# Keys of the second layer and keys and values of the third made inside feed-forward sections

## The reference, cut to what matters

```
# second layer (weights L1_*): pruned attention, then a ternary feed-forward
kh = heads(ctx @ Wk.T + bk);  vh = heads(ctx @ Wv.T + bv)
p  = softmax(qh kh^T / 4); the 14 keys with the least column sum are dropped
x  = x + concat(p vh) @ Wo.T + bo
x  = x + bitlinear(gelu(bitlinear(layernorm(x), w1, b1)), w2, b2)
# third layer (L2_*): masked attention
K = heads(ctx @ Wk.T + bk);   V = heads(ctx @ Wv.T + bv)
p = softmax(where(mask, Q K^T / 4, -1e9));  x = x + concat(p V) @ Wo.T + bo
```

## Time and profile before

| what | us |
|---|---|
| median of 3 runs (lowest, highest) | 1206.9 (1205.46, 1210.3) |
| the profiled execution's own time | 1207.3 |
| its span | 1205.3 |
| PE busy | 1015.1 (84%) |
| DVE busy | 900.0 (75%) |
| ACT busy | 755.9 (63%) |
| POOL busy | 238.1 (20%) |

### The profile page before, as it was taken

How to read it: one execution, slowest core, us unless ns; L and a number is a source line. 1 busy time by engine, 2 the same in 40 slices (tenths; PEclk the granted TensorE clock), 3 DMA queues, 4 the chain that set the end, 5 groups by cost and what they waited for, 6 DMA issues and landing times. The chain is left out here.

```text
span 1205.3 us, 28063 instructions
## 1 busy us (share of the span) xinstructions
PE 1015.1 (84%) x9190; PEld 824.6 (68%) x9190; DVE 900.0 (75%) x2541; ACT 755.9 (63%) x2804; POOL 238.1 (20%) x426
## 2 busy tenths in 40 slices
PE   3999967578999976667999978999998993888885
PEld 3788855246777753446777758999997982666663
DVE  4789868786888868995777765566556984788884
ACT  2787887577777868885777753112113552688884
POOL 1233310002222212332223210000001111333331
PEclk8899998858999997887999999999998996799998
DMA  7340000000000000004232000000000100000002
GB/s 241 92 143 17 14 1 1 1 9 15 14 13 13 10 2 1 0 0 106 76 87 62 13 2 1 1 0 0 0 1 18 32 23 1 1 2 0 0 1 70
DMA packets 44426, 32.64 MB, mean 27 GB/s; under 512 B 16184, under 2 KB 43456, under 8 KB 44352
## 3 DMA queue, kind: packets, MB, share of 16 engines
q1 hardware_dynamic: 44352, 31.72, 8.8%
HBM read 23.32 MB, written 2.10 MB: 21 GB/s over the span
## 5 line engine op out<-in xcount | busy, mean ns | idle before, releaser
L783 ACT ACTIVATE L1a_pr<-L1a_scores,L1a_nm 128x128 f32<-128x128 f32 x256 | 93.1, 417 | 13.5 <-DVE L1a_nm L857 13.5
L783 ACT ACTIVATE L2a_pr<-L2a_scores,L2a_nm 128x128 f32<-128x128 f32 x256 | 90.9, 392 | 5.8 <-DVE L2a_nm L857 5.8
L783 ACT ACTIVATE L3f_pr<-L3f_scores,L3f_nm 128x128 f32<-128x128 f32 x256 | 90.5, 403 | 3.3 <-DVE L3f_nm L857 3.3
L783 ACT ACTIVATE L0a_pr<-L0a_scores,L0a_nm 128x128 f32<-128x128 f32 x256 | 90.9, 392 | 2.3 <-DVE L0a_nm L857 2.3
L783 ACT ACTIVATION_READ_ACCUMULATOR L1a_pr<-L1a_scores,L1a_nm 128x1 f32 x256 | 65.5, 256 | 0.0
L783 ACT ACTIVATION_READ_ACCUMULATOR L3f_pr<-L3f_scores,L3f_nm 128x1 f32 x256 | 62.4, 244 | 0.0
L2145 POOL TENSOR_TENSOR x_all<-x_all,L3a_xnorm 128x256 f32<-128x256 f32 x16 | 11.9, 743 | 253.6 <-DVE L3a_nm L2164 253.6
L857 DVE TENSOR_REDUCE L2a_nm<-L2a_scores 128x4 f32<-128x512 f32 x64 | 42.2, 682 | 25.2 <-PE L2a_scores L644 25.2
L1789 PE MATMUL L2f_inner<-L2f_taT,L2f_loraBT 128*128 128x128 f32 x512 | 59.7, 275 | 0.9 <-DVE L2f_hs L1941 0.9
L1778 PEld LDWEIGHTS L2f_inner<-L2f_xTb,L2f_wiT 128*128 128x128 f32 x512 | 58.3, 192 | 1.5 <-ACT L2f_loraBT L1745 1.2
L1778 PE MATMUL L2f_inner<-L2f_xTb,L2f_wiT 128*128 128x128 f32 x512 | 58.6, 275 | 0.9 <-ACT L2f_loraBT L1745 0.9
(11 more groups left out here) (550 smaller groups left out, 3050.7 us busy)
## 6 DMA issues: line engine op xcount, KB each, us to landing
setup_ctx_nat<-in_ctx SPq DMA_DIRECT2D x4, 512.0 KB, 5.5
x_all<-in_x SPq DMA_DIRECT2D x1, 2048.0 KB, 12.4
L0a_ctxT<-ctxT_all SPq DMA_DIRECT2D x16, 128.0 KB, 2.0
L_ffn_w_w<-in_L_ffn_w SPq DMA_DIRECT2D x2, 1024.0 KB, 7.0
L1a_ctxT<-ctxT_all SPq DMA_DIRECT2D x16, 128.0 KB, 2.0
L2a_ctxT<-ctxT_all SPq DMA_DIRECT2D x16, 128.0 KB, 2.0
L3a_mem<-in_ctx SPq DMA_DIRECT2D x16, 128.0 KB, 2.0
out<-x_all SPq DMA_DIRECT2D x1, 2048.0 KB, 7.5
```

The costliest lines, as they stand in the source:

```text
L783: ex = act.activation(pr[q.s][:, j, h, :], S[j][:, h * P:h * P + P], ACT.Exp, bias=nm[q.s][:, j, h:h + 1], scale=-1.0, accum_out=ls[q.s][: ...
```

## The change

- L0f: TensorE transposes the second layer's Wk at the section's start, VectorE copies it and splits the bias row bk into three bf16 rows (`BiasRows.vector`, placed ahead of the normalization of x). After slots 5, 8, ..., 20 TensorE makes the keys of two sequences each (`project_keys`: for each sequence four products in f32 and two in bf16 that add the bias), the last four sequences' keys after slot 23; ScalarE copies each pair's keys (128x512) to SBUF. ScalarE's square root for the layer norm goes ahead of its weight scaling.
- L1a: no `project_k`, `add_k` or transposed Wk; `kbd` comes from the stored keys. The rounding of the ternary weights is split: `scale` after `drop_eight`, `clip` where `add_k` was, `round` after `add_q`.
- L1f: Wk and Wv of the third layer are transposed after the ternary weights, the 512-wide bias row is split on VectorE ahead of the first normalization, and in each pair step TensorE makes keys and values of two sequences (`keys_values`) into one bank `KV`, which ScalarE copies (128x512) twice in a step (`take_kv`). That bank comes out of `T2`: three banks A, B, C now hold the transposed h of both streams, and stream 1 waits until ScalarE has taken stream 0's. TensorE's loop is written out.
- L2a: no `project_k`, `project_v`, `add_k`, no context copies; `add_v` is a copy from the stored values; SyncE issues all later loads without waits. Wk and Wv aren't transposed here.
- First-layer weights, the eight-bit weights and, later, the stored keys and values share one SBUF area (`arena`).

```diff
 # L1a, vector
                         piece(prev, drop_eight)
+                        if cur:
+                            beside.scale(dve, cur.b)
                         piece(last, norm_out)
                         piece(prev, drop_rest)
                         piece(nxt, add_k)
+                        if cur:
+                            beside.clip(dve, cur.b)
                         piece(last, add_out)
                         piece(nxt, add_q)
+                        if cur:
+                            beside.round(dve, cur.b)
                         piece(prev, keep_values)
...
-                    if kind == PRUNED and cur:
-                        beside.round(dve, cur.b)
 # the bias, vector
+        dve.memset(self.parts, 0.0).then_inc(self.s, 1)
+        dve.wait_ge(self.s, n)
+        src = self.row
+        for k, at in enumerate((0, 32, 64)):
+            dve.tensor_copy(piece, src).then_inc(self.s, 1)
...
+            dve.tensor_copy(self.parts[at:at + 1, :], piece[at:at + 1, :])
+            ins = dve.tensor_tensor(rest, src, piece, ALU.subtract)
...
 # L0f, tensor
+                def project_keys(m, bank):
...
+                    for s in range(NS):
+                        for j in range(DC):
+                            out = bank[:, s * D + j * P:s * D + j * P + P]
+                            for c in range(DC):
+                                pe.matmul(out, WkT[:, c, j * P:j * P + P], g.ctxT[:, NS * m + s, c, :],
+                                          start=(c == 0), stop=False)
+                            mm = bias.keys(pe, g, out, j * P)
+                    mm.then_inc(s_k_ps, 1)
...
                         mm.then_inc(s_gu_ps, 1)
-                    if i == 0:
-                        pe.wait_ge(s_t_sb, NL + FLAT)
+                        if FC0 * i + f in key_slots:
+                            project_keys(key_slots[FC0 * i + f], banks[6])
+                pe.wait_ge(s_h, FC0 * NG - 2)
+                for n in range(2):
+                    project_keys(6 + n, banks[n])
 # L1f, scalar
                             act.activation(hh[s][:, :], hp[s][:, :], ACT.Gelu).then_inc(s_gelu[s], 1)
+                            if nxt and s == 0:
+                                take_kv(nxt, 0)
+                    if nxt and not cur:
+                        take_kv(nxt, 0)
...
                     if old:
                         turn_back(old, 1, 0).then_inc(s_qT[1][1], 1)
+                    if nxt:
+                        take_kv(nxt, 1)
 # L1f, tensor
+                def keys_values(b):
+                    if b:
+                        pe.wait_ge(s_kv, b)
+                    for j in range(DC):
+                        out = KV[:, j * P:j * P + P]
+                        for c in range(DC):
+                            pe.matmul(out, WkT[:, c, j * P:j * P + P], g.ctxT[:, b, c, :], start=(c == 0), stop=False)
+                        bias.keys(pe, g, out, j * P)
+                    out = KV[:, D:2 * D]
+                    for c in range(DC):
+                        pe.matmul(out, g.ctxT[:, b, c, :], WvT[:, c, :], start=(c == 0), stop=False)
+                    bias.values(pe, g, out, D).then_inc(s_kv_ps, 1)
+
                 def step(old, cur, nxt):
+                    if nxt:
+                        keys_values(nxt.b(0))
                     if old:
                         for s in range(NS):
                             pe.wait_ge(s_scaled[1][s], old.v)
                             pe.wait_ge(s_x[s], old.v)
+                            if s == 1:
+                                pe.wait_ge(s_qT[1][0], old.v)
...
                                 mm = pe.transpose(XT[s][:, c * P:c * P + P], xs[s][:, c * P:c * P + P], g.ident[:, :])
                             mm.then_inc(s_qT_ps[0][s], 1)
+                        keys_values(nxt.b(1))
```

More of the change, by code:

```diff
@@ L443, with attention @@
 COPIES = {PLAIN: "vvav", PRUNED: "aaaa", MASKED: "vvav", MIXED: "vvav"}
-def attention(nc, g, name, kind, w, turned, needs, later=(), beside=None):
+def attention(nc, g, name, kind, w, turned, needs, later=(), beside=None, keys=None, vals=None):
     sec = Section(nc, name)
@@ L601, in project, with bank_free @@
                     return mm
-                def project_k(q, new, prev):
+                def bank_free(q, new, prev):
                     if new:
@@ L743, in fill @@
                 def fill():
[L744 to L748, removed]
+                    for k in ("Wk", "Wv"):
+                        if turned and k in turned:
+                            turn_weight(k)
+                    if not no_k:
+                        w_turned(pe, "Wk")
+                        project(w["Wk"], g.ctxT[:, 0]).then_inc(s_k_ps[0], 1)
                     for s, bank in ((0, T[1]), (1, G)):
@@ L1138, in factors, with scale, clip, round @@
         dve.reciprocal(self.inv, self.mean.unsqueeze(2).to_broadcast([P, 2, NB // 2]))
-    def round(self, dve, k):
+    def scale(self, dve, k):
         row, scale = self.rows[:, k, :], self.inv.rearrange("p w k -> p (w k)")[:, bass.ds(k, 1)]
         dve.tensor_scalar(row, row, scale, MAGIC, ALU.mult, ALU.add).then_inc(self.s_scaled, 1)
+    def clip(self, dve, k):
+        row = self.rows[:, k, :]
         dve.wait_ge(self.s_scaled, k + 1)
         dve.tensor_scalar(row, row, MAGIC + 1.0, MAGIC - 1.0, ALU.min, ALU.max).then_inc(self.s_clipped, 1)
+    def round(self, dve, k):
         dve.wait_ge(self.s_clipped, k + 1)
-        dve.tensor_scalar(self.rounded[:, k, :], row, MAGIC, None, ALU.subtract)
-def fake_quant_ffn(nc, g, w, q8, q3):
+        dve.tensor_scalar(self.rounded[:, k, :], self.rows[:, k, :], MAGIC, None, ALU.subtract)
+class BiasRows:
+    def __init__(self, nc, sb, name, width):
+        self.width = width
+        self.row = sb(f"{name}_row", [P, width])[:, :]
+        self.parts = sb(f"{name}_parts", [P, width], BF16)[:, :]
+        self.s = nc.alloc_semaphore(f"{name}_split")
+    def vector(self, dve, rest, piece):
+        n = 1
+        dve.memset(self.parts, 0.0).then_inc(self.s, 1)
[3 more added lines that the diff above has]
+            dve.tensor_copy(piece, src).then_inc(self.s, 1)
+            n += 1
+            dve.wait_ge(self.s, n)
+            dve.tensor_copy(self.parts[at:at + 1, :], piece[at:at + 1, :])
+            ins = dve.tensor_tensor(rest, src, piece, ALU.subtract)
+            ins.then_inc(self.s, 1)
+            n += 1
+            dve.wait_ge(self.s, n)
+            src = rest
+        self.count = n
+    def keys(self, pe, g, out, lo):
+        return pe.matmul(out, self.parts[0:96, lo:lo + P], g.onesb[0:96, :], start=False, stop=True)
+    def values(self, pe, g, out, lo):
+        return pe.matmul(out, g.onesb[0:96, :], self.parts[0:96, lo:lo + D], start=False, stop=True)
+def fake_quant_ffn(nc, g, w, q8, q3, Wk, bias, keys):
     sec = Section(nc, "L0f")
@@ L1253, in _, with take_keys @@
                 load_table(act, g, ACT.Silu)
+                def take_keys(m, bank):
+                    act.wait_ge(s_k_ps, m + 1)
+                    act.copy(keys[:, NS * m:NS * m + NS, :, :], bank[:, :].rearrange("p (b c t) -> p b c t", b=NS, c=DC)
+                             ).then_inc(s_k, 1)
                 for i in range(NG):
@@ L1386, in _, with bitlinear_ffn @@
                 sweep_pairs(pe, step)
-def bitlinear_ffn(nc, g, w, q3):
+def bitlinear_ffn(nc, g, w, q3, wkv, bias, both):
     sec = Section(nc, "L1f")
@@ L1472, in _, with take_kv @@
                              .rearrange("p (m n) -> p m n", m=4)).then_inc(s_t_sb, 1)
+                for n, (dst, bank) in enumerate(((WkT, A), (WvT, B))):
+                    act.wait_ge(s_kw_ps, n + 1)
+                    act.copy(dst[:, :, :], bank[:, :].rearrange("p (c n) -> p c n", c=DC)).then_inc(s_kw, 1)
+                def take_kv(q, s):
+                    act.wait_ge(s_kv_ps, NS * q.v + s - 1)
+                    act.copy(both[:, q.b(s), :], KV[:, :]).then_inc(s_kv, 1)
                 def turn_back(q, s, m):
```

176 lines of the change are left out of this document (131 added, 45 removed).

## The result

The kernel after takes 1245.3 us (median of 4 runs, 1242.4 to 1248.0), the kernel before 1208.2 beside it (4 runs): ratio 1.031, 95% interval 1.0275 to 1.0341. It is slower, as forecast, but by 37 and not by 22, and 5 above the end of the range. The profiled execution has a span of 1243.1, 37.8 more than before.

The account below looks back on a forecast made before the run. The prediction took the chain of engines setting each section's pace as the bound, reading one steady step per changed section. Its terms summed to +22.6: 1207.3 + 22.6 = 1229.9, less 0.4, rounded down to 1229 us; range 1210 to 1240.

Parts of the forecast that it names:

- 1. L0f, start: L0f's start: earlier square root saves 2.0, VectorE's copy of Wk and bias split cost more; net +1.7 us.
- 2. L0f, slots: L0f's slots: key products exceed TensorE's free time and set the pace, groups 4.6 apart; +5.0 us.
- 3. L1a: L1a: earlier minima shorten steps, missing project_k gives nothing, fill loses 1.2; -5.7 us in all.
- 4. L1f, start: L1f's start: bias split, first keys and values and their copy delay scaling of x; +7.8, second step +2.8 us.
- The step that failed: L1f's six full steps: added copies and two waits make 13.2, with some half clock 13.6 on average; +15.9 us.
- The ends: L1f's last two steps: they wait likewise, +1.5 us.
- 6. L2a: L2a: without project_k and project_v ScalarE sets steps of 8.96 against 9.29, fill gives 1.4; -6.4 us.
- Rival B: L1f: half clock meets every pair step, six times 1.6 more than the forecast; 1239 us, chance 0.12.
- Rival A: L0f and L1f: TensorE's added work hides better, L1f steps 12.5; 1215 us, chance 0.22.
- rival C: Both attention sections: TensorE is the true pace, each removed product counts; faster, 1198 us, chance 0.05.
- rival D: Whole kernel: work moves and time doesn't; attention -17, L0f +3, L1f +14; 1207 us, chance 0.09.

Follow-up runs that it names:

- e2: Kernel before with only L1a's rounding split into scale, clip and round, keys still made in L1a: 1200.4 us, ratio 0.9914 to 0.9963.
- e3: Kernel after without its L0f part, so L1a makes its own keys again, all else kept: 1238.6 us.
- e7: As e3 with e1's order in L1f; biases of keys and values added by VectorE in L2a, without bias split and bias products: 1214.1 us.
- e4: Kernel after, with the second sequence's keys and values made once more, unused, between the streams' transposes in L1f's six full steps: 1236.7 us.
- e6: Kernel after, with 16 unused f32 products added on TensorE at the start of L1a and of L2a: 1244.9 us.
- b3: As e7, with sequences shifted so L1f's first step makes no keys or values, plus 16 unused products at L2a's start: 1199.8 us.
- e1: Kernel after, TensorE's L1f order alone changed: second sequence's keys and values between the streams' transposes, x's transposes ahead of stream 1's: 1227.0 us.
- e5: Kernel after, with only the second sequence's keys and values moved between the streams' transposes in L1f: 1230.6 us.

## Why the prediction was wrong

Its direction held, and so did the waits that it named; what the half clock costs behind them was priced too low. Point by point:

1. L0f, start: +1.7 forecast, +1.6 measured (first maxima).
2. L0f, slots: +5.0 forecast, +6.4. (The 0.3 that is left of the table's 8.3 is no time: VectorE's normalization row now stands ahead of the one that scales weights.) Keys of two sequences took 2.17 and not 2.0, so groups are 4.76 apart and not 4.6. Of the first slots one more ran at the low clock, 1.0 more.
3. L1a: the steps gave 5.4 for a forecast 4.5, and e2 shows that all of it is the split. That `project_k` gives nothing is shown by e3. The fill was forecast 1.2 shorter and was 1.1 longer, at a granted clock of 0.63 where it had been 0.80; with its key products back (e3) it is as before in both. The end, which had no term, was 0.7 longer: the last output product, after the same 0.92 of idle time, took 2.08 and not 1.13.
4. L1f, start: the first `xs` was 7.7 later for a forecast 7.8, which is in part luck. That it waits for the first keys and values at the low clock was right. But what holds these is the wait for the turned Wk and Wv, which had no term, and the split of the bias only 0.5 beyond it: without the split and the bias products (e7) `xs` is still 6.5 later than before, and the start as long as in e3. To the second step's end +14.2 for a forecast 10.6: in the second step, too, the products between x's transposes and the hidden ones ran at 1.2 GHz (1.06 + 1.17 for the keys), and I had priced them at 2.4.
5. **The step that failed**: "Sum 13.2; some steps at half clock, 13.6 on average". The 13.2 without the clock is right (13.3 in two of the steps, and in all six of e4). But four of six steps ran slow, and each of them lost 1.4 to 2.8 by it, 8.5 in all, where I had put 6 x 0.4 = 2.4. An average of 0.4 at my price of 1.6 is a quarter of the steps; it was two thirds of them, at 2.1 on average. I priced the slow clock by the transposes of h and x alone, and the keys and values that stand behind them on TensorE, for which ScalarE waits next, are slow as well. This part (22.7 for 15.9) and the start (14.2 for 10.6) are 10.4 of the 17.0 by which the four sections went over the forecast; L2a is 2.6 of it, L1a 2.2, L0f 1.6, L1f's end 0.2. The ends were +1.7 for +1.5.
6. L2a: steps as forecast. The fill gained 0.1 and not 1.4, and the second step was 1.2 longer, both at the low clock, as e6 shows.

Rival B named the right mechanism but not its extent. It had all six steps at 15.2; two ran at 13.3 and four at 15.4 on average, so the six took 88.4 where B gives 91.2. That the kernel came out above B's 1239 lies elsewhere: the clock also took the gains of both fills, for which neither the forecast nor B had a term. For L2a's fill e6 and b3 show it; in L1a's the added products ran low themselves, so there it rests on the granted clock (0.63 for 0.80) and on e3, where both came back. Rival A fell with the order of the waits, rival C with the earlier trace rows, whose 8.96 came out, and rival D since both attentions together gave 7.3 and not 17. That the idle time of TensorE wasn't where the new products stood, my reason against A, is what e1 confirms: once the products were moved into the idle time, the six steps lost 1.9 and not 22.7.

## What to carry to other kernels

Work moved under another section is paid by its place in the order, not by its length. On each in-order engine, ask what stands behind the new instruction and which wait it brings forward; in this kernel the same products cost 22.7 or 1.9 in six steps. Put moved work into the gap that the waits leave on its engine, where it also keeps the clock up. And when an edit opens a gap of some 3 us on TensorE, price all that stands behind the gap until the engine is fast again at half speed; where work is taken away from a section's start, look there too.

## What the runs showed of the hardware

More work on TensorE made a stretch shorter, in three runs. With 2.15 of unused products in each of six gaps the six steps took 8.5 less and the kernel 8.6 less (e4). With 16 unused products at its start L2a took 4.3 less (e6) and 5.1 less (b3). The same idle time before stream 1's transposes, 3.26 or 3.27, was followed in the kernel after by the low clock in three steps and by the high one in two; 4.63 was followed by the low one, and 0.82 in e4 and e5 by the high one. A short idle time doesn't guarantee the high clock either: after 0.92 the last output product of L1a took 1.13 in the kernel before and in e4, and 2.08 in the kernel after. In L1a the same filler at the section's start didn't help: it ran low itself.
